# Attention outputs of four head couples in one PSUM bank, the two heads of a couple in the same 32 rows

## The reference, cut to what matters

```
scores = einsum('bhqd,bhkd->bhqk', q, k) / sqrt(8)
attn   = softmax(scores)
out    = einsum('bhqk,bhkd->bhqd', attn, v)      # q: 128 queries, k: 128 or 77 keys, d: 8
x      = x + out.reshape(..., 128) @ Wo + bo
```

## Time and profile before

| | us |
|---|---|
| median of 3 runs | 2819.55 |
| lowest and highest | 2813.89 and 2821.55 |
| span of the profiled execution | 2821.3 |

### The profile page before, as it was taken

One profiled execution on the slowest core, in us unless ns is written; L12 is line 12 of the kernel. 1 busy time (PEld: TensorE's weight loads), 2 busy tenths in 40 slices (PEclk: granted clock), 3 DMA queues, 4 the chain that ended last, 5 costly groups with the idle time before them and its releaser, 6 DMA issues. The chain is left out here.

```text
span 2821.3 us, 71603 instructions
## 1 busy us (share of the span) xinstructions
PE 2444.5 (87%) x28224; PEld 1716.4 (61%) x28224; DVE 1547.7 (55%) x4577; ACT 1585.2 (56%) x2443; POOL 548.9 (19%) x726
## 2 busy tenths in 40 slices
PE   3656989898989999898989999898989999888975
PEld 2434657575766657575766657575766657565643
DVE  3343555656475565656475565657475565734232
ACT  1324555666665665666665665666666665645432
POOL 2111111221212122121212121121212121111111
PEclk9756989999999999999999999999999999998975
DMA  2100011111020111111020111111020101010000
GB/s 112 34 16 19 18 27 30 26 31 33 23 44 23 37 25 30 26 31 33 23 44 23 39 23 28 28 31 33 23 44 23 43 19 34 22 25 17 17 20 17
DMA packets 103757, 84.30 MB, mean 30 GB/s; under 512 B 15000, under 2 KB 102681, under 8 KB 102937
## 3 DMA queue, kind: packets, MB, share of 16 engines
q1 hardware_dynamic: 103449, 79.91, 12.1%
HBM read 14.21 MB, written 4.19 MB: 7 GB/s over the span
## 5 line engine op out<-in xcount | busy, mean ns | idle before, releaser
L978 DVE TENSOR_REDUCE smax<-by_query_banks 128x8 f32<-128x616 f32 (+1 forms) x512 | 515.9, 1008 | 326.7 <-PE by_query_banks L1294 325.9
L764 ACT ACTIVATE probs<-by_key_banks 77x1024 f32<-77x1024 f32 (+1 forms) x512 | 518.4, 1012 | 208.9 <-PE by_key_banks L1316 205.4
L746 ACT ACTIVATE hid<-by_query_banks,cols 128x512 f32<-128x512 f32 x512 | 334.6, 686 | 270.7 <-PE by_query_banks L1222 269.0
L1231 PEld LDWEIGHTS by_key_banks<-moe_w,hid 128*128 128x128 f32 x4096 | 476.0, 192 | 14.1
L1231 PE MATMUL by_key_banks<-moe_w,hid 128*128 128x128 f32 x4096 | 483.7, 275 | 0.0
L1364 PE MATMUL weighed_bank<-probs,values 128*32 128x128 f32 x8192 | 362.5, 300 | 2.6 <-ACT probs L764 1.9
L1294 PE MATMUL by_query_banks<-k_int,q_int 32*128 32x128 f16 (+1 forms) x4096 | 197.6, 218 | 139.4 <-DVE smax L978 76.9
L1294 PEld LDWEIGHTS by_query_banks<-k_int,q_int 32*128 32x128 f16 x4096 | 119.5, 98 | 301.4 <-issue 194.9
L1364 PEld LDWEIGHTS weighed_bank<-probs,values 128*32 128x32 f32 x8192 | 209.7, 116 | 94.9 <-issue 44.4
L1316 PE MATMUL by_key_banks<-q_int,k_int 32*128 32x128 f16 x4096 | 221.4, 231 | 4.9 <-ACT probs L764 4.6
L966 DVE SCALAR_TENSOR_TENSOR x_s<-by_key_banks,gates,x_s 128x128 f32<-128x128 f32 x512 | 143.2, 342 | 129.4 <-PE by_key_banks L1231 129.4
(11 more groups left out here) (232 smaller groups left out, 3824.2 us busy)
## 6 DMA issues: line engine op xcount, KB each, us to landing
q_int<-q_nat SPq DMA_DIRECT2D x256, 128.0 KB, 2.7
k_int<-k_nat SPq DMA_DIRECT2D x128, 128.0 KB, 2.7
k_int<-k_nat SPq DMA_DIRECT2D x128, 77.0 KB, 2.3
x_tok<-in_x SPq DMA_DIRECT2D x17, 256.0 KB, 3.0
q_int<-m_sb SPq DMA_DIRECT2D x256, 4.0 KB
out<-res SPq DMA_DIRECT2D x16, 256.0 KB, 2.3
ctx_tok<-in_ctx SPq DMA_DIRECT2D x17, 154.0 KB
hid<-in_moe_w SPq DMA_DIRECT2D x1, 2048.0 KB
```

Source lines behind the costliest of these rows:

```text
L746: act.activation(hidden[e % 2][:, c, :], A[c % 2], ACT.Gelu, bias=col(f"moe_b1_{e}_{c}")).then_inc(S["gelu"], 1)
L764: act.activation(probs[h % 2][0:nk], by_key[0:nk], ACT.Exp, scale=DH ** -0.5)\
L978: dve.tensor_reduce(smax[h // 2 % 2][:, pair, :], scores, AX.X, ALU.max, negate=True)\
L1231: last = pe.matmul(B[e % 2][:, seq_tok(b)], hidden[e % 2][:, c, seq_tok(b)], moe_w2[:, e, c, :], start=(c == 0), stop=(c == CHUNKS - 1))
```

## The change

The values of a couple of heads get 18 columns for each head: the even head has its 8 values in columns 0 to 7 and its one in column 16, the odd head has its 8 values in columns 8 to 15 and its one in column 17; the other columns are zero. Both heads' products go to the same 32 rows and the same 128 columns of `O`, the second added to the first (`start=k == 0, stop=k == 1`). So `O` holds four units, and the copy, the four turnings, the reciprocals and `o_norm` come once for four units. Each time there is one copy, four turnings, one reciprocal over 32 elements and two products of 128 elements. ScalarE writes the values with two instructions in place of one. The strings in `TURNS` lose the letters of the phases that are gone; the other phases keep their order among each other on every engine, but that on TensorE at the end of the step the last `back` now stands behind `query1` and `value1`.

```diff
-VC = DH + 1
+COUPLE = 2 * DH
+VC = COUPLE + 2
+BLOCK = 4
+BLOCKS = 2
...
-                elif c % 2:
-                    yield f"{kind}{m}_{c // 2}", kind, m, c // 2
-                if kind == "weigh" and c % 2:
-                    yield f"copy{m}_{c // 2}", "copy", m, c // 2
+                elif kind == "max" and c % 2:
+                    yield f"max{m}_{c // 2}", kind, m, c // 2
+                elif kind == "back" and c % BLOCK == BLOCK - 1:
+                    yield f"back{m}_{c // BLOCK}", kind, m, c // BLOCK
+                if kind == "weigh" and c % BLOCK == BLOCK - 1:
+                    yield f"copy{m}_{c // BLOCK}", "copy", m, c // BLOCK
...
-        ones = [x.v[0:nk, :, :, DH:] for x, nk in zip(att, KEYS)]
+        ones = [x.v[0:nk, :, k::2, COUPLE + k] for x, nk in zip(att, KEYS) for k in range(2)]
...
-                act.activation(att[m].v[0:nk, :, :, 0:DH],
-                               X[1][0:nk, :].rearrange("k (b h d) -> k b h d", b=GROUP, h=HEADS), ACT.Copy)\
-                    .then_inc(S["proj_sb"], 1)
+                values = X[1][0:nk, :].rearrange("k (b c h d) -> k b c h d", b=GROUP, c=COUPLES, h=2)
+                for k in range(2):
+                    last = act.activation(att[m].v[0:nk, :, k::2, DH * k:DH * k + DH], values[:, :, :, k, :], ACT.Copy)
+                last.then_inc(S["proj_sb"], 1)
...
-                        act.wait_ge(S["pv"], at(g, "pv", 2 * (h + 1)))
+                        act.wait_ge(S["pv"], at(g, "pv", BLOCK * (h + 1)))
...
-                        dve.reciprocal(o_rden[j % 2][:], o_t[:, :, :, DH]).then_inc(S["o_rden"], 1)
+                        dve.reciprocal(o_rden[j % 2][:], o_t[:, :, :, COUPLE:VC]).then_inc(S["o_rden"], 1)
                         dve.wait_ge(S["o_rden"], at(g, "o_rden", j + 1))
-                        dve.tensor_tensor(x.o_norm[:, :, rows_of(j)].rearrange("q b (i d) -> q i b d", d=DH),
-                                          o_t[:, :, :, 0:DH],
-                                          o_rden[j % 2][:].unsqueeze(3).broadcast_to([P, SLOTS, GROUP, DH]),
-                                          ALU.mult).then_inc(S["o_norm"], 1)
+                        half = x.o_norm[:, :, j * D // BLOCKS:(j + 1) * D // BLOCKS]
+                        for k in range(2):
+                            last = dve.tensor_tensor(half.rearrange("q b (i k d) -> q i b k d", i=BLOCK, k=2)[:, :, :, k, :],
+                                                     o_t[:, :, :, DH * k:DH * k + DH],
+                                                     o_rden[j % 2][:, :, :, k].unsqueeze(3).broadcast_to([P, BLOCK, GROUP, DH]),
+                                                     ALU.mult)
+                        last.then_inc(S["o_norm"], 1)
...
-                        if h % 2 == 0 and o_free:
+                        if h % BLOCK == 0 and o_free:
...
-                            i, at_head = 2 * (h % 2) + k, VC * (2 * h + k)
+                            at_head = VC * (2 * h + k)
                             for b in range(GROUP):
-                                last = pe.matmul(O[VW * b:VW * b + VW, i * T:(i + 1) * T],
+                                last = pe.matmul(O[VW * b:VW * b + VW, h % BLOCK * T:(h % BLOCK + 1) * T],
                                                  x.v_wide[:, b, at_head:at_head + VW], probs[h % 2][:, k, seq_tok(b)],
-                                                 start=True, stop=True)
+                                                 start=k == 0, stop=k == 1, skip_group_check=True)
```

More of the change, by code:

```diff
@@ L109 @@
 TURNS = {
-    "PE": "iiiiiihxlhhxxxllhlhllhhllhxlhlhllhhxhhlhhllxhhhlhlhhllhhlllhhhhxxxhhhhhhxhxhxhhhhhhxhhhhhhhhhhhx"
-          "hhhhhhhhhxhhhhhhhhhxhhhhhhhhhxhhhhhhhhhxhhhhhhhxxxhhhhhhhhhhhhhhhhhxhhhhhhhhhhhhxxhhhhhhxhxxxhhh"
-          "hhhhhhhhhhhhhxhhhhhxhhhhhxxxxxhhhxxxhhhhhhhhhhhhxhhxxhxh",
+    "PE": "iiiiiihxlhhxxxllhlhllhhllhxlhlhllhhxhhlhhllxhhhlhlhhllhhlllhhhhxxxhhhhhhxhxhxhhhhhhxhhhhhhhhhhxh"
+          "hhhhhhhxhhhhhhhhxhhhhhhhhxhhhhhhhhxhhhhhhxxxhhhhhhhhhhhhhhhxhhhhhhhhhhhxxhhhhhxhxxxhhhhhhhhhhhhh"
+          "hhxhhhhxhhhhxxxxxhhhxxxhhhhhhhhhhxhhxxxh",
@@ L113 @@
     "ACT": "iiiihxxxxhhllllhhhhllllhxlhhhlllhxhhhllhlllhhhhhhhxlllllhhhhhhhhhhhhhiixxxxxhhhxhhhhxhhhhhhhhhhh"
-          "hxhhhhhhhhhxhhhhhhhhhhhxhhhhhhhxhhhhhhhhhxxxxhhhhhhhhhhhhhhhhhhhhhhhhhhhxxhhhhhhhhhhhhhhxxxxxhhh"
-          "hhhhhhhhhhhhhhhxhhhhxxxxxhhhhxxxxhhhhhhhhhhhhhhhhxxhhhxx",
+          "xhhhhhhhhxhhhhhhhhhhxhhhhhhxhhhhhhhhxxxxhhhhhhhhhhhhhhhhhhhhhhhhxxhhhhhhhhhhhhxxxxxhhhhhhhhhhhhh"
+          "hhhxhhhhxxxxxhhhxxxxhhhhhhhhhhhhhhxxhhxx",
     "DVE": "lllxhhxhhhhxxxlllllllilhhhhxllhhhhhhhhilllllhhhhlllhhhhlxxxhhhhhhxxhhhhhhhhxhhxxxhhhhhhhhhhhhhhh"
-          "hhhhhhhhhhhxhhhhhhhhhxxxhhhhhhhhhhhhhhhhhhhhhhxxhhhhhhhhhxhhhhhhhhhhhhhhxhhhhxhhhhhxxhhhhxxhhhhh"
@@ L118 @@
-          "hhhhxxxhhhhhhhhhhhhhhhhhhhhxxxxxxhhhhhhxxxiiihhhhhxhxxhi",
+          "hhhhhhhhxhhhhhhhhxxxhhhhhhhhhhhhhhhhhhhhxxhhhhhhhhxhhhhhhhhhhhhxhhhhxhhhhxxhhhhxxhhhhhhhhxxxhhhh"
+          "hhhhhhhhhhhhhhxxxxxxhhhhxxxiiihhhhhxxxhi",
     "POOL": "llllllllllxxhhhhhhhhhhhhhhhhhhhhhhhhhhhhhhhhhhhhhhhhhhhhhhhhhhhhhhhhhhhhhhhhhhhhhhhhhhhhhhhhhhhh"
-          "hhhhhhhhhhhhhhhhhhhhhhhhhhhhhhhhhhhhhhhhhhhhhhhhhhhhhhhhhhhhhhhhhhhhhhhhhhhhhhhhhhhhhhhhhhhhhxxx"
-          "llllllllllllxxxxxxixxxxxxxxxiiiixxxxxxxxxxxxxxxxxxxxxxxi",
@@ L122 @@
-    "SP": "iiiiiillllllxxxxxhhhhhhhhhhhhhhhhhhhhhhhhhhhhhhhhhhhhllllllllllllllllxxxxxxhhhxhhhhhhhhhhhhxxxhh"
-          "hhhhhhhhhhhhhhhhhhhhhhhhhhhhhhhhhhxxxxxxxxxxxxxxxxxxxhhhhhhhhhhhhhhhhhhhhhhhhhhhhhhhhhhhhhhhhhhh"
-          "hhhhhhhhhhhhhhhhhhhhhhhhhhhhhhhhhhhhhhhhhhhhhhhxxxxxxxxx",
+          "hhhhhhhhhhhhhhhhhhhhhhhhhhhhhhhhhhhhhhhhhhhhhhhhhhhhhhhhhhhhhhhhhhhhhhhhhhhhhxxxllllllllllllxxxx"
+          "xxixxxxxxxxxiiiixxxxxxxxxxxxxxxxxxxxxxxi",
+    "SP": "iiiiiillllllxxxxxhhhhhhhhhhhhhhhhhhhhhhhhhhhhhhhhhhhhllllllllllllllllxxxxxxhhhxhhhhhhhhhhhxxxhhh"
+          "hhhhhhhhhhhhhhhhhhhhhhhhhhhhhxxxxxxxxxxxxxxxxxxxhhhhhhhhhhhhhhhhhhhhhhhhhhhhhhhhhhhhhhhhhhhhhhhh"
+          "hhhhhhhhhhhhhhhhhhhhhhhhhhhhhhhxxxxxxxxx",
@@ L346, in build @@
         o_sb = [sb(f"o_sb{i}", [P, N]) for i in range(2)]
-        o_rden = [sb(f"o_rden{i}", [P, SLOTS, GROUP]) for i in range(2)]
+        o_rden = [sb(f"o_rden{i}", [P, BLOCK, GROUP, 2]) for i in range(2)]
         moments = {n: Moments(n + "_") for n in ("ctx", "x", "layers", "light")}
@@ L1242, in heavy @@
                     b_free = [("probs", p, COUPLES)] * 2
-                    o_free, z_free = ("o_sb", p, TILES), ("o_norm", p, TILES)
+                    o_free, z_free = ("o_sb", p, BLOCKS), ("o_norm", p, BLOCKS)
                 if r.b:
@@ L1375, in heavy @@
                             pe.wait_ge(S[sem], at(p, sem, count))
-                        for i in range(SLOTS):
+                        for i in range(BLOCK):
                             last = pe.transpose(Z[:, i * T:(i + 1) * T], o_sb[h % 2][:, i * T:(i + 1) * T], ident[:])
```

8 lines of the change are left out of this document (4 added, 4 removed).

## The result

The changed kernel took 2836.0 us (2830.87 to 2842.03, 11 runs) against 2824.5 us of the kernel before on the same chip: ratio 1.0044, interval [1.0031, 1.0057]. So it is slower by 0.2 to 0.45%, some 5 to 12 us. The forecast was 2814 us, the range 2788 to 2835. The profiled execution spans 2834.1 us at a mean granted clock of 0.913; that of before 2821.3 us at 0.923.

What follows compares the result with a forecast made beforehand. The prediction took the last-ending wait to bound each head iteration, not TensorE; -0.7 us over 14 steps and -5 us at start and end gave a span of 2815.6 us, hence a median of 2814 us, range 2788 to 2835.

Steps and rivals of the forecast that it cites:

- What bounds: Head stage: TensorE's 87% misleads; the wait that ends last sets each iteration, in even ones the turned maxima behind VectorE.
- VectorE's longer reading: Each `back` that stays: reciprocal 0.10 us longer, second product 0.20 us more, so `Z` is released 0.30 us later.
- The sum over a step: Gains and losses of the iterations and stage's end nearly cancel: -0.05 us a step, -0.7 us in 14.
- The end of the stage: End of a step's head stage: the shorter queue on VectorE was to gain 0.08 us a step.
- Start and end, -5 us: Where an attention runs alone, half the `back`s go: 1.6 us gained for each of three attentions, 5 us.
- The experts' part: The rest of a step beside the heads: claimed not to be entered by the change, so given no term.
- The clock: Slower rival: thinner work makes cross-attentions lose the clock for two iterations each, +28 us, 2845 us; chance 0.05.
- The sign given for it: Iterations 7 to 16 in the profile after: a clock under 1.00 in most steps would show the clock rival.
- The second head waits for the first: Slower rival: adding in the bank makes `weigh` 0.4 us longer in 512 places, perhaps a tenth seen: 2834 us; chance 0.03.
- the waits go and don't come back: Faster rival: six middle `back`s that go return 0.38 us each, those kept hide their longer work: 2784 us; chance 0.17.
- TensorE is the bound after all: Faster rival: all 79 us of the turnings removed from TensorE are gained, 2741 us; chance 0.04.
- the third rival: Slower: iterations 12, 16, 20, 24 pay the longer `back` in full, gains in 10 and 14 lost: 2832 us; chance 0.11.

Runs made afterwards that it cites:

- b_slow: Kernel before plus one more 128x128 VectorE product, read by nothing, in every second reading of a turned bank: 2841.01 us, ratio 1.0049.
- a_short: Changed kernel with VectorE's reading halved (reciprocal of 128x16, one product for two; odd heads not divided): 2807.25 us, ratio 0.9934.
- a_fill_mid: Changed kernel plus four unit-matrix turnings, read by nothing, behind the weighed sums of each of the first six blocks: 2824.94 us, ratio 1.0002.
- b_thin: Kernel before with two of each bank's four turnings left out, VectorE reading one turned block for all four: 2803.57 us, ratio 0.9923.
- b_end: Kernel before plus one 128x128 VectorE product behind module 2's second reading of a turned bank, ahead of the stage's last addition: 2823.22 us, ratio 0.9999.
- b_thin_slow: Kernel before with two of four turnings left out and an extra VectorE product in every second reading: 2818.26 us, ratio 0.9979.

## Why the prediction was wrong, point by point

- *What bounds.* Right: TensorE's share misleads, and the path of the even iterations runs over `Z`, VectorE and the turned maxima. `b_slow` and `a_short` show it directly.
- *VectorE's longer reading.* Right in size. The reciprocal took 353 ns for 355 forecast: (353 - 255) / 16 = 6.1 ns an element. The second product follows at 0.20 us, and the hold grew by 0.29 us for 0.30. The estimate of 8.3 ns an element, from what the Trainium skill ("VectorE: DVE Perf Modes", section "First, the fixed hardware budget") says of the divide, would have given 388 ns; the measurement decides.
- *The sum over a step.* Nearly right, at full clock: iteration 10 by -0.46 (-0.38 forecast), 14 by -0.31 (-0.20), 12 and 16 by +0.30 each (+0.30), 20 and 21 together by +0.10 (+0.15), 24 to 27 by -0.22 (-0.15), though with 24 itself by +0.03 only (+0.30) and 25 by +0.20. The heads came to -0.36 us, iteration 23 left out, where the forecast's terms for them made +0.03. With the end a step at full clock is 0.1 us the better (0.05 forecast). Hits and misses of up to 0.3 us stand behind the small sum, so its closeness is in part luck. What it hides is how much hangs on the reading: 0.20 us more of it in every second `back` cost 14 us (`b_slow`).
- *The end of the stage.* The first step that failed: "at the stage's end the shorter queue on VectorE gives 0.08". It lost 0.24. The queue has one reading less, but the reading left stands directly ahead of L952, as in the timeline of VectorE before and after:

```profile
1991.23 0.24 DVE L985 RECIPROCAL o_rden<-turned_bank 128x16 f32<-128x16 f32 x1
...
1991.50 0.29 DVE L987 TENSOR_TENSOR o_norm<-turned_bank,o_rden 128x128 f32<-128x128 f32 x1
1991.71 0.53 DVE L946 SCALAR_TENSOR_TENSOR k_nat<-light_bank,cols,k_nat 128x308 f16<-128x308 f32 x1
```

```profile
1682.55 0.34 DVE L991 RECIPROCAL o_rden<-turned_bank 128x32 f32<-128x32 f32 x1
...
1682.93 0.49 DVE L995 TENSOR_TENSOR o_norm<-turned_bank,o_rden 128x128 f32<-128x128 f32 x2
1683.33 0.53 DVE L952 SCALAR_TENSOR_TENSOR k_nat<-light_bank,cols,k_nat 128x308 f16<-128x308 f32 x1
...
1683.91 0.87 PEld L1418 LDWEIGHTS light_bank<-mats,cakv_f 128*77 128x77 f32 x8 [1.49 <-DVE k_nat L952]
```

  It is 0.32 us a step beside the forecast, 4.5 us in 14.
- *Start and end, -5 us.* The second, and larger. The start came out 5.7 us longer (482.8 us for 477.1; again 484.6 for 472.9) at a clock of 0.79 for 0.81, the end 0.6 us longer. In the end the stage before the last gained 2 us (141.1 for 143.3 us) and the last lost 2.4 at a clock of 0.73 for 0.77; the latter didn't repeat. The forecast gain, if it is there, is covered by the clock. With the 6.6 us of the 13 steps these make the profiled difference of 12.8 us.
- *The experts' part.* The third: "the experts' part, which this change doesn't enter". Its products are the same as before (483 and 482 are recorded in the clean steps), and it lost 8.3 us in the 13 steps by its clock.
- *The clock.* What the second and third have in common, and the decisive term: the sum had nothing for it. It was a rival at 0.05, with the wrong picture: the cross-attentions would drop to the lower level in two iterations each and show it there. Iterations 7 to 16 are at 1.00 in the clean step, and yet the mean clock fell from 0.924 to 0.914, because the start has more low time and more of the expert parts have a low stretch. The sign given for it, a clock under 1.00 in iterations 7 to 16, couldn't tell: iterations 7 and 8 are under 1.00 in 9 of 13 steps of either kernel, 10 to 16 in nearly none, and the step of the earlier trace rows, where iteration 7 is at 1.00, was one of the few. By the slope of 0.22 us the fall is worth 13 us. With -2 us for 14 steps at full clock and -2 us for the stage before the last the sum is +9 us; measured were +12 and +5. `a_fill_mid` has only more work on TensorE, and gets 0.010 of clock back. With that agrees the rule of the Trainium skill ("TensorE: Matmul & The Clock Gate", section "What's actually happening") that activity releases the throttle, which should have weighed more. It alone isn't enough either: `b_thin` has as few turnings as the changed kernel and lost only 0.003, and `b_end`, with nothing more on TensorE, won 0.005.
- *The rivals.* "The second head waits for the first" fell (300 ns a product before, 301 after), "the waits go and don't come back" too (iterations 12 and 16 are longer), and "TensorE is the bound after all" (the odd iterations stayed at 1.6 us). The measured 2836 us are near the third rival's 2832, but not for its reason: iterations 10 and 14 kept their gain. The clock's 2845 us is mis-added: 28 us on the forecast are 2842.

What stays open: why the changed kernel's clock is lower (0.914 and 0.916) than that of `b_thin_slow` (0.918) and `b_thin` (0.921) with equally many turnings, and why its low stretches fall into the experts' part, where they cost twice as much. These leave their turnings spread over 16 places and the changed kernel has them in 8; it also adds in the bank, and copies and writes values otherwise. No run takes these apart. The difference in time between the changed kernel and `b_thin_slow`, 11 to 18 us, is assigned in part only: by the slope 2 to 5 us are the clock's, and the reading is 0.1 us longer still, by `b_slow`'s rate (14 us for 0.20) 7 us. In the one profile of `b_thin_slow` the rest lies in the steps, where its expert parts kept their clock; one profile doesn't show that this is the rule.

## What to carry to other kernels

A bank that two chains share is a resource of its own: count how long each holds it, from the first write to the last read, even where both engines have room, since 0.20 us more of a hold by a half-idle engine, in every second reading, were 14 us here (`b_slow`), and two of four turnings fewer ahead of every reading were 20 (`b_thin`). When several small works are merged into one, look for what stands directly behind the merged one on its engine (here a projection's addition, cured by a change of order). And where a kernel shows stretches at either clock level, take the mean clock over many runs of both kernels before trusting a sum of iterations at full clock, and look for the low stretches in the parts that the change doesn't enter too. A clean step is one sample: compare it with its neighbours before a tenth of a us is read from it.

## What the runs showed of the hardware

- Products that compute nothing can shorten a kernel: 384 turnings of the unit matrix more, 5 to 12 us less by the two comparisons, mean clock from 0.914 and 0.916 to 0.924.
- The same program's mean granted clock varied from 0.918 to 0.930 between runs, and its time with it, by 0.22 us for each us of low time; the scatter between its runs (2814 to 2832 us) is in good part this.
- What a us of low time costs depends on the place: 0.49 us in the experts' part, where TensorE is busy for 64.0 of 64.9 us, and 0.23 us in the heads.
- A reciprocal on VectorE takes 255 ns for 16 and 353 ns for 32 elements of each partition.
- Adding a second product to rows just written in the bank cost nothing: 300 ns a product before, 301 ns after.
